# Shared feed-forward stage of a decoder layer: rows of five batches turned by VectorE after a trip through DRAM, and a new order of the work around it

## The reference, cut to what matters

```
xf      = layernorm(x)
shared  = gelu(xf @ Wfc_s + bfc_s) @ Wproj_s + bproj_s
logits  = xf @ Wr;  the two largest of 8 are chosen, their gates sum to 1
routed  = sum over the two experts e of gate_e * (gelu(xf @ Wfc[e] + bfc[e]) @ Wproj[e] + bproj[e])
out     = x + shared + routed
```

## Time and profile before

| | us |
|---|---|
| median of 3 runs | 917.37 (916.71 to 919.80) |
| the profiled execution | 916.98 |
| its span, first to last instruction | 915.3 |
| PE busy (matmuls) | 886.2 (97%) |
| DVE busy | 625.2 (68%) |
| ACT busy | 524.0 (57%) |
| POOL busy | 331.0 (36%) |

### The profile page before, as it was taken

How to read it: one execution, slowest core, us unless ns; L and a number is a source line. 1 busy time by engine, 2 the same in 40 slices (tenths; PEclk the granted TensorE clock), 3 DMA queues, 4 the chain that set the end, 5 groups by cost and what they waited for, 6 DMA issues and landing times.

```text
span 915.3 us, 20404 instructions
## 1 busy us (share of the span) xinstructions
PE 886.2 (97%) x6734; PEld 778.9 (85%) x6743; DVE 625.2 (68%) x1465; ACT 524.0 (57%) x1050; POOL 331.0 (36%) x318
## 2 busy tenths in 40 slices
PE   8999998999998999999999999999999999999996
PEld 6688995566554888888988999999999999999996
DVE  5998696899877776666656766575665657575553
ACT  4683434556455655446444775575766667575552
POOL 3477222211302555555553224232232323322222
PEclk9999999999999999999999999999999999999998
DMA  9300020000002111111226556335353533533332
GB/s 251 121 1 1 2 92 1 2 1 1 1 7 94 51 54 67 66 61 67 84 95 224 141 114 145 47 54 128 48 131 47 139 47 47 139 47 47 47 47 35
DMA packets 87855, 64.00 MB, mean 70 GB/s; under 512 B 58112, under 2 KB 80832, under 8 KB 87680
## 3 DMA queue, kind: packets, MB, share of 16 engines
q0 software_dynamic: 17504, 34.87, 16.5%
q1 hardware_dynamic: 60192, 26.80, 11.5%
q10 hardware_dynamic: 10112, 1.70, 1.1%
HBM read 38.58 MB, written 24.77 MB: 69 GB/s over the span
## 4 chain that ended last, share of the span: by engine, by line
PE 79%; DVE 7%; DMA 4%; ACT 4%; issue 4%; POOL 1%; SPq 0%; ACTq 0%; DVEq 0%; POOLq 0%
PE PS L137 22%; PE PS L139 21%; PE PS L138 21%; DMA metar<-routed_rows 3%; PE PS L894 3%; PE PS L309 2%; PE PS L924 2%; PE PS L938 1%; PE PS L944 1%; ACT hideh L1913 1%; DVE mxpad L1138 1%; PE PS L1402 1%; ACT act32e L1915 1%; PE PS L1384 1%; DMA win<-in_W_inT 1%
## 5 line engine op out<-in xcount | busy, mean ns | idle before, releaser
L1944 POOL DMA_INDIRECT out_rows<-y,toki x70 | 113.5, 1622 | 265.9 <-DVE y L1974 246.6
L1913 ACT ACTIVATE hideh<-PS,be 128x256 fp32r<-128x256 f32 x280 | 143.7, 513 | 101.3 <-PE PS L139 101.2
L143 DVE TENSOR_TENSOR hidel<-act32e,hideh 128x256 fp32r<-128x256 f32 x280 | 118.0, 425 | 84.0 <-ACT act32e L1915 81.6
L137 PE MATMUL PS<-xTeh,wfch 128*128 128x256 f32 x560 | 158.6, 283 | 1.9 <-ACT act32e L1915 1.1
L137 PE MATMUL PS<-wprh,hideh 128*128 128x256 f32 x560 | 158.5, 283 | 1.9 <-DVE hidel L143 1.9
L138 PE MATMUL PS<-xTel,wfch 128*128 128x256 f32 x560 | 157.6, 281 | 0.0
L139 PE MATMUL PS<-xTeh,wfcl 128*128 128x256 f32 x560 | 157.5, 281 | 0.0
L139 PE MATMUL PS<-wprh,hidel 128*128 128x256 f32 x560 | 156.5, 279 | 0.0
L138 PE MATMUL PS<-wprl,hideh 128*128 128x256 f32 x560 | 156.3, 279 | 0.0
L1915 ACT ACTIVATE act32e<-PS,be 128x256 f32<-128x256 f32 x280 | 144.6, 516 | 8.7 <-DVE hidel L143 8.1
L137 PEld LDWEIGHTS PS<-wprh,hideh 128*128 128x128 f32 x560 | 104.9, 187 | 5.2 <-DVE hidel L143 4.9
(11 more groups left out here) (273 smaller groups left out, 2059.8 us busy)
## 6 DMA issues: line engine op xcount, KB each, us to landing
xb<-routed_rows SPq DMA_DIRECT2D x144, 64.0 KB
fcraw<-in_Wfc POOLq DMA_DIRECT2D x8, 1024.0 KB, 6.0
prraw<-in_Wproj POOLq DMA_DIRECT2D x8, 1024.0 KB, 9.0
out_rows<-X SPq DMA_DIRECT2D x8, 512.0 KB, 2.9
X<-in_x SPq DMA_DIRECT2D x7, 512.0 KB, 7.6
routed_rows<-pads SPq DMA_DIRECT2D x8, 272.0 KB, 4.3
out_rows<-y,toki POOLq DMA_INDIRECT x70, 3.8
ctx<-in_ctxT SPq DMA_DIRECT2D x4, 256.0 KB, 7.1
```

The lines of the kernel that those rows point to most:

```text
L137: nc.tensor.matmul(out, wh, xh, start=first, stop=False)
L143: return eng.tensor_tensor(out, whole, high.bitcast(F32), ALU.subtract)
L1913: nc.scalar.activation(hid[0][:, j, :], PS[:, j % 4, 0:BLK], ACT.Gelu_apprx_tanh, bias=bias)
L1944: nc.gpsimd.indirect_dma_start(out=out, out_offset=bass.IndirectOffsetOnAxis(ap=toki[:, h:h + 1], axis=0), in_=y[:, h, :], in_offset=None, ...
```

## The change: what it does

For the batches 2 to 6 (all but `DIRECT`, 0, 1 and 7) the eight PE transposes go. SP writes `hn` to a DRAM buffer `HN` (512 KB, 1 KB runs), waits for it, and reads it back by four DMAs, one for each quarter of the partitions, in runs of 256 B, into `xq`. One DVE instruction (`turn`, 128x1024 f32, blocks of 32x32) writes the turned rows into PSUM banks 4 and 5. The order of the features that comes out is not the natural one, so the rows of `Wfc_s` and `Wr` are permuted outside the kernel, and for the direct batches `apply_permuted` writes `hn` in that order and `copy_rows` undoes it by four ACT instructions in place of one.

With it comes another order in the periods b = 1 to 5 (`whole_turned`). PE does up 2 to 7 without a break, then down 0, logits, down 1, transpose_logits, down 2 and 3, ranks, up 0 and 1. ACT does `evac(b+1)` between slices 5 and 6 and the logits, the copy of the rows and the gates after slice 7. DVE does stats between slices 3 and 4, the turn between 4 and 5, x_low after 5, then `apply_part(b+2)` ahead of `choose(b+1)`, both residuals, and the placing of b+1 after ranks, with the low parts of slices 0 and 1 of b+1 between its steps.

```diff
+        HN = nc.dram_tensor("batch_rows", [L, D], F32, kind="Internal").ap()
...
+            xq = Place(wfc1_at)("xq", [P, L // SQ, KD, SQ])
+            xq_in, = phase_sems(ctx, "c_xq_in")
+            XQ_IN = 16 * (1 + P // SQ)
+            DIRECT = (0, 1, B - 1)
+            FIRST = 2
             def shared_sync(sp):
+                def quarters(b):
+                    sp.wait_ge(hn_ready, b + 1)
+                    sp.dma_start(HN.rearrange("(t p) d -> p t d", p=P), hn[:]).then_inc(xq_in, 16)
+                    sp.wait_ge(xq_in, XQ_IN * (b - FIRST) + 16)
+                    for q in range(P // SQ):
+                        sp.dma_start(xq[q * SQ:(q + 1) * SQ].rearrange("p t k i -> p t (k i)"),
+                                     HN[:, q * KD * SQ:(q + 1) * KD * SQ].rearrange("(t j) c -> j t c", j=SQ)).then_inc(
+                                         xq_in, 16)
...
                 for b in range(B - 2):
+                    if b + 2 not in DIRECT:
+                        quarters(b + 2)
                     store(b)
...
             def shared_tensor(pe):
...
+                def whole_turned(b, first=2):
+                    up(b, range(first, KH))
+                    down(b, range(1))
+                    logits(b + 1)
+                    down(b, range(1, 2))
+                    transpose_logits(b + 1)
+                    down(b, range(2, TB))
+                    ranks(b + 1)
+                    up(b + 1, range(2))
...
-                    whole(b)
+                    (whole if b + 1 in DIRECT + (B,) else whole_turned)(b)
...
             def shared_scalar(act):
...
-                    nc.scalar.activation(rows[:, :, 0:D], hn[:], ACT.Copy).then_inc(hn_copied, 1)
+                    if b in DIRECT:
+                        for t in range(TB):
+                            last = nc.scalar.activation(
+                                rows[:, t, 0:D].rearrange("p (q k i) -> p q k i", k=KD, i=SQ),
+                                hn[:, t, :].rearrange("p (k q i) -> p q k i", k=KD, i=SQ), ACT.Copy)
+                    else:
+                        last = nc.scalar.activation(rows[:, :, 0:D], hn[:], ACT.Copy)
+                    last.then_inc(hn_copied, 1)
...
+                def whole_turned(b, first=2):
+                    gelus(b, range(first, 6))
+                    evac(b + 1)
+                    gelus(b, range(6, KH))
+                    if b == B // 2:
+                        act.wait_ge(raw_in, 32)
+                        for k in range(KD):
+                            split_up(0, k)
+                        split_down(0)
+                    evac_logits(b + 1)
+                    copy_rows(b + 1)
+                    gates(b + 1)
+                    gelus(b + 1, range(2))
...
             def shared_vector(dve, routed_first):
...
+                def turn(b):
+                    dve.wait_ge(xq_in, XQ_IN * (b - FIRST + 1))
+                    dve.wait_ge(lT_ready, b)
+                    nc.vector.transpose(PS[:, 4:4 + KD, :].rearrange("p k (t j) -> p t k j", j=SQ),
+                                        xq[:]).then_inc(hT_psum, 1)
...
+                def place(b):
+                    place_rows(b)
+                    lows(b, range(1))
+                    for m in range(2):
+                        place_slots(b, m)
+                    lows(b, range(1, 2))
+                    place_gates(b)
+
+                def whole_turned(b, first=2):
+                    lows(b, range(first, 4))
+                    stats_part(b + 2)
+                    lows(b, range(4, 5))
+                    turn(b + 1)
+                    lows(b, range(5, 6))
+                    x_low(b + 1)
+                    lows(b, range(6, KH))
+                    apply_part(b + 2)
+                    choose(b + 1)
+                    residual(b, range(2))
+                    place(b + 1)
```

More of the change, by code:

```diff
@@ L1275, in build @@
             wfc = [tmp("wfc" + n, [P, 2, KD, HID], F32R) for n in "hl"]
+            wfc1_at = tmp.at - 2 * 4 * 2 * KD * HID + 4 * KD * HID
             wpr = [tmp("wpr" + n, [P, 2, KH, D], F32R) for n in "hl"]
@@ L1620, in apply_part, with apply_permuted @@
                     dve.wait_ge(hn_rstd, 2 * b + 2)
-                    norm_apply(b).then_inc(hn_ready, 1)
+                    (apply_permuted if b in DIRECT else norm_apply)(b).then_inc(hn_ready, 1)
+                def apply_permuted(b):
+                    for t in range(TB):
+                        last = nc.vector.tensor_scalar(
+                            hn[:, t, :].rearrange("p (k q i) -> p k q i", k=KD, i=SQ),
+                            X[:, TB * b + t, :].rearrange("p (q k i) -> p k q i", k=KD, i=SQ), mv[:, t, 0:1],
+                            rstd[:, t:t + 1], ALU.subtract, ALU.mult)
+                    return last
                 def first_of(score, top, choice):
@@ L1713, in next_rows @@
                     dve.wait_ge(att_hT_psum, 2 * B)
-                    norm_apply(0).then_inc(hn_ready, 1)
+                    apply_permuted(0).then_inc(hn_ready, 1)
                 def next_split():
@@ L1774, in shared_vector @@
                 for b in range(1, B - 1):
-                    whole(b)
+                    (whole if b + 1 in DIRECT else whole_turned)(b)
                 dve.wait_ge(e_high, 2 * KD)
@@ L2094 @@
         "bv": nd(L0_xattn_bv).reshape(-1, P).T, "bo": nd(L0_xattn_bo).reshape(1, -1),
-        "Wfc_s": nd(L0_ffn_Wfc_s), "bfc_s": nd(L0_ffn_bfc_s).reshape(-1, P).T,
+        "Wfc_s": nd(L0_ffn_Wfc_s).reshape(4, D // P, P // 4, HID).transpose(1, 0, 2, 3).reshape(D, HID),
+        "bfc_s": nd(L0_ffn_bfc_s).reshape(-1, P).T,
         "Wproj_s": nd(L0_ffn_Wproj_s), "bproj_s": nd(L0_ffn_bproj_s).reshape(1, -1),
-        "Wr": nd(L0_ffn_Wr), "Wfc": nd(L0_ffn_Wfc).reshape(E, 4, D // P, P // 4, HID).transpose(0, 2, 1, 3, 4).reshape(E, D, HID),
+        "Wr": nd(L0_ffn_Wr).reshape(4, D // P, P // 4, E).transpose(1, 0, 2, 3).reshape(D, E), "Wfc": nd(L0_ffn_Wfc).reshape(E, 4, D // P, P // 4, HID).transpose(0, 2, 1, 3, 4).reshape(E, D, HID),
         "bfc": nd(L0_ffn_bfc).reshape(E, -1, P).transpose(2, 0, 1),
```

## The result

The changed kernel takes **932.81 us** (median of 4 runs, 930.17 to 936.89), the kernel before beside it 918.3: a ratio of 1.0175, 95% interval 1.0149 to 1.0201 (the two medians alone give 1.0158, 14.5 us). The forecast was 932.0. The profiled execution of after took 933.11 us, with a span of 931.5 against 915.3 before: 16.2 us to be found.

What follows compares the result with a forecast made beforehand. PE, busy 25.00 of 25 us in the shared stage, bounds the kernel. Period 1 +3.6, b = 2 to 5 +10.8, period 6 +0.2: +14.6 on 916.98 is 931.6, median 0.4 higher: 932.0 (929 to 936, chance 0.50).

Steps and rivals of the forecast that it cites:

- The turn path: Turn, evac, gelus and low parts delay slices 6 and 7 in down 0: 1.7 and 0.8 us, period 26.5.
- The loop: Scatters, copy of rows, normalising, choice, ranks and placing wait on each other: 27.6 us, setting the steady periods.
- the choice is not slowed: Rival: choice on DVE not slowed by POOL's adds, loop 26.0, turn's path 26.5 rules: 927.6; chance 0.22.
- Period 1: First turned period: the DRAM trip has no cover, 28.3 to 28.5 us, +3.6 (bounds +1.6 and +6).
- the trip: hn through DRAM to xq: write 2.9, reads 7.4 us (4.9 to 9.8); uncovered in period 1, covered in steady periods.
- The clock: Rival: PE's clock falls after the stalls in down 0, +0.5 to +1.6 over five periods: 934 to 938; 0.08 with dear turn.
- Period 6: Period with the old order, entered with DVE behind by the placing: +0.2 us.
- Wait before ranks: PE waits about 1.1 us before ranks for the choice, moved there from the first path's stalls.
- The routed stage "as before, shifted": Routed stage starts as before, shifted with PE, its first rows waiting for batch 7's scatters.
- The other side, at 913: Rival: turn ends before about 9.7, loop below 24.0, neither binds, 0.88 us kept each period: 913.0; chance 0.12.

Runs made afterwards that it cites:

- changed_again: The changed kernel itself, unaltered, timed again beside the kernel before: 929.73 us, ratio 1.0159.
- choice_first: The changed kernel with choose(b+1) ahead of apply_part(b+2) on DVE in the five turned periods: 929.23 us, ratio 1.0156 to the kernel before.
- adds_late: The kernel of evac_late with POOL's bias adds waiting for the end of the choice: 924.21 us, ratio 1.0101 to the kernel before.
- turned_best: The changed kernel with choose ahead of apply_part, evac behind slice 7, stats, logits and ranks later, period 5 handing over to the old order: 915.84 us, ratio 1.0002.
- evac_late: The changed kernel with ACT's evac behind the gelu of slice 7 and DVE's x_low behind its low part: 937.63 us, ratio 1.0237.

## Why the prediction was right, point by point

The 16.2 us of span, by the same matmuls in both traces: -1.05 ahead of up 0 of batch 1 (325.99 against 327.04), +14.96 in the five periods, +1.2 in period 6, +1.1 behind it. The forecast had 0, 14.4, 0.2 and 0. The first is no effect of the change: up 0 of batch 1 starts between 323.4 and 328.6 in the profiles of all these kernels, which, the kernel before apart, differ only behind it, and the 327.04 of before lies in that range. The medians, 14.5 us apart on that chip and 14.1 on the other (changed_again), stand nearer to the forecast's 14.6 than the two profiles do.

- **The turn path: right.** The turn takes 1.25 us (1.3 taken), and ACT waits 2.21 for it. DVE, ACT, period 3:

```profile
393.00 1.25 DVE L1717 STREAM_TRANSPOSE PS<-xq 128x1024 f32<-128x1024 f32 x1
...
394.28 1.09 ACT L1521 ACTIVATE xT0h<-PS 128x512 fp32r<-128x512 f32 x2 [2.21 <-DVE PS L1717]
```

  It ends 11.9 us after up 0 (394.25 less 382.35), the number forecast. PE's waits are 1.33 to 1.80 and 0.53 (1.7 and 0.8). Alone it gives 26.25 to 26.7 (choice_first; 26.5).
- **The loop: right**, in each term and in the sum. (The 5.59 us named in the prediction are ACT's wait for the scatters, not the slack that the change gives up: that is from the end of the copy to the normalising, 4.95 us by rows 3 and 6.) Placing ready 6.85 (6.65), send 11.65 to 12.19 (11.9), landing 1.5, copy 1.06, normalising 1.38 with the choice starting 1.30 after it, choice 4.55 to 4.67 (4.72); 27.3 to 27.7 where the clock stays up. So the rival *the choice is not slowed* falls, and adds_late shows what it would have been worth.
- **Period 1: size near, cause wrong.** The step that failed is the trip: I took 10.3 us from hn to xq (2.9 + 7.4), it was 7.7. SP's write and reads, and DVE, after:

```profile
328.55 0.38 SPq L1355 DMA_DIRECT2D batch_rows<-hn  x1
331.53 1.92 SPq L1358 DMA_DIRECT2D xq<-batch_rows  x4
```

```profile
336.25 1.26 DVE L1717 STREAM_TRANSPOSE PS<-xq 128x1024 f32<-128x1024 f32 x1 [0.17 <-DMA xq<-batch_rows]
```

  The write took 3.0 as its row said; the reads took 4.7 from first issue, like the first routed load with half as many runs: my lower bound, not the middle. xq came as DVE was free for it, and period 1 was set by the loop as the others, 27.84 in place of 28.4 (+2.95, not +3.6). The scatters didn't start "where they did" either: POOL's adds ahead of them took 4.19 in place of 3.74 us and the scatters 12.19 in place of 11.9, so that the loop held ranks at 27.7 and not at the 27.2 of the forecast.
- **The clock: the rival came true inside the forecast.** Its place was right, behind the waits of down 0, and its cost in one period too: periods 2 and 3 are 1.1 and 0.8 longer than the loop's 27.4, where it had 1.6 less the 1.1 hidden, 0.5 to 1.6. What it made of that was wrong: over five periods these are 2.5 to 8 us, 934.5 to 940 and not 934 to 938. It was given little weight for the shorter gaps, and it does occur in some periods only. Against the forecast's terms, periods 2 and 3 came out 1.5 us dearer, periods 1, 4 and 5 1.0 cheaper. The total is so close because these errors cancelled.
- **Period 6: wrong**, +1.2 for +0.2, the mis-sized term of the sum. The placing of batch 6 now lies beside up of batch 6, ahead of the low parts, where the old order placed between down 2 and 3. All kernels with that hand-over show some of it (0.6 to 2.2 us from up 0 of batch 6 to ranks of 7). The two largest have a clock of 0.94 in that period. turned_best hands over in the old way, and takes 47.97 us from up 0 of batch 6 to the first routed matmul against 47.87 before; but its fifth period is 1.0 longer than before, so the cost has moved and not gone.
- **Wait before ranks: too large**, forecast about 1.1, measured 1.35, 0, 0, 0.41 and 0.54. The turn path is 26.7 in place of 26.5, the loop 27.4 in place of 27.6, so 0.7 is left where the clock stays up, and nothing behind a fall. The wait is the difference of the two paths, not a cost of its own.
- **The routed stage "as before, shifted": open.** From the first to the last scatter of results it took 393.8 us against 392.9. In the other turned kernels it was 392.9 to 395.4, in the two without a turn 392.0 and 392.4. A cause wasn't tried.
- **The other side, at 913:** fell. It needed both paths to be over 2 us shorter; where the clock stays up, they were within 0.3 of the forecast.

## What to carry to other kernels

A step that is moved behind another on an in-order engine takes over that one's waits. Before such a move follow the releases across the iterations: here copy, normalising, choice, ranks, placing and scatters had slack only because the choice stood ahead of the normalising. Where two paths are nearly equal, each edit alone shows almost nothing, so try them together before dropping either; and ask what a moved semaphore now starts, and beside what (POOL's adds beside the choice, 1.55 us a period). Removing 0.88 us from a full engine is worth at most that, and costs more as soon as a wait of 2 us comes up in its place.

## What was not expected of the hardware

- **A fall of the clock is not certain.** The same 2.2 us of idle PE in 5 us were followed by 0.55 and 0.57, or by 1.00 (rows above). A fall costs 1.4 us where nothing hides it, and about as much although PE waits before ranks, if it lies on the way to what the loop waits for (evac_late, 8.2 for 6.85 us).
- **Scatters land late now and then:** 1.5 us from the end of the last issue to ACT's copy in most batches, 2.5 to 3.8 in one or two batches of ten of the thirteen profiles. The cause wasn't sought. The order before has 4.95 us of slack for it, and a landing of 3.23 us in batch 3 left its period at 24.9; a loop without slack pays all of it.
- **DVE's transpose into PSUM** goes at a pace like that within SBUF: 1.25 us for 128x1024 against 0.704 for 128x512.
